# A four-block convolution network on one core: borders cleared alone, an up layer's weights prepared a stage earlier, x blocks loaded first, and loops written out

## The reference

```python
# L0: windowed attention, 8x8 windows, 8 heads, and an MLP with a hidden width of 768
h = layernorm(xw, ln1_g, ln1_b);  q, k, v = split(h @ qkv_w)
a = softmax(q k^T * scale) v @ proj_w + proj_b + xw
x = gelu(layernorm(a, ln2_g, ln2_b) @ fc1_w + fc1_b) @ fc2_w + fc2_b + a
# L1: Sobel edges in x and y, a 1x1 convolution of 384 to 192 channels, layernorm, gelu, residual
x = x + gelu(layernorm(conv1x1(edges(x))) * ln_w + ln_b)
# L2: 7x7 depthwise convolution, layernorm, up layer (w1) to 768, gelu, response norm, down layer (w2)
y = gelu(layernorm(depthwise7x7(x, dw_w) + dw_b) @ w1 + b1)
x = x + (grn_gamma * (y * nx) + grn_beta + y) @ w2 + b2     # nx from sums of y^2 over each image
# L3: 13x13 depthwise convolution and six dilated ones, each with a batch norm, summed
```

## Time and profile before

| | |
|---|---|
| median of 3 runs | 3580.73 us (3580.53 to 3581.01) |
| the profiled execution | 3581.64 us, of which the span from the first to the last instruction 3579.5 us |
| mean granted TensorE clock | 0.98 of full speed |
| TensorE busy | 3423.4 us (96%) |
| VectorE, ScalarE, GpSimd busy | 2389.3 (67%), 1790.2 (50%), 1080.1 us (30%) |
| transfers | 554.97 MB, 155 GB/s over the span |

### The profile page before, as it was taken

One profiled execution on the slowest core, in us unless ns is written; L12 is line 12 of the kernel. 1 busy time (PEld: TensorE's weight loads), 2 busy tenths in 40 slices (PEclk: granted clock), 3 DMA queues, 4 the chain that ended last, 5 costly groups with the idle time before them and its releaser, 6 DMA issues. The chain is left out here.

```text
span 3579.5 us, 95798 instructions
## 1 busy us (share of the span) xinstructions
PE 3423.4 (96%) x31958; PEld 3312.3 (93%) x31958; DVE 2389.3 (67%) x5936; ACT 1790.2 (50%) x5312; POOL 1080.1 (30%) x1951
## 2 busy tenths in 40 slices
PE   7999999999799999999969969989999899989999
PEld 6888888888699999999969969989999899989999
DVE  5777777777556666666659979979999311125554
ACT  4666666666444444444426657659999200002222
POOL 3233333333244444444425520014444223320000
PEclk9999999999899999999989989999999899999999
DMA  1455566610011111111158865537777788877775
GB/s 34 123 197 192 198 239 235 233 58 23 23 34 51 51 51 51 50 51 51 50 141 256 247 188 198 196 124 201 198 198 199 221 253 253 251 228 228 227 227 174
DMA packets 472671, 554.97 MB, mean 155 GB/s; under 512 B 78259, under 2 KB 331957, under 8 KB 472373
## 3 DMA queue, kind: packets, MB, share of 16 engines
q1 hardware_dynamic: 447028, 531.65, 49.3%
q10 hardware_dynamic: 25344, 19.27, 1.7%
HBM read 392.56 MB, written 271.52 MB: 186 GB/s over the span
## 5 line engine op out<-in xcount | busy, mean ns | idle before, releaser
L1325 PE MATMUL PS<-dw_grid,dw_mats 128*128 128x196 f32 (+1 forms) x3840 | 624.0, 326 | 37.0 <-DVE dw_mats L1266 37.0
L1325 PEld LDWEIGHTS PS<-dw_grid,dw_mats 128*128 128x128 f32 x3840 | 623.5, 191 | 37.5 <-DVE dw_grid L1262 37.5
L1297 ACT ACTIVATE dw_res<-PS,dw_brow 128x196 f32<-128x196 f32 x192 | 81.5, 424 | 699.3 <-PE PS L1325 699.3
L981 PE MATMUL PS<-mlp_w,mlp_hid 128*128 128x192 f32 x2352 | 414.0, 326 | 0.5 <-ACT mlp_hid L796 0.5
L1262 DVE COPY dw_grid<-X 32x392 f32 (+3 forms) x480 | 290.3, 605 | 171.8 <-PE PS L1325 148.7
L1560 PE MATMUL PS<-gain,down_hid 128*128 128x192 f32 x2352 | 385.4, 328 | 3.6 <-DMA down_hid<-scratch_hid 3.6
L1560 PEld LDWEIGHTS PS<-gain,down_hid 128*128 128x128 f32 x2352 | 385.1, 191 | 3.9 <-DMA down_hid<-scratch_hid 3.9
L981 PEld LDWEIGHTS PS<-mlp_w,mlp_hid 128*128 128x128 f32 x2352 | 378.3, 190 | 0.8 <-ACT mlp_hid L796 0.8
L796 ACT ACTIVATE mlp_hid<-PS,mlp_b 128x256 f32<-128x256 f32 x588 | 247.0, 471 | 110.8 <-PE PS L787 110.8
L1187 PE MATMUL PS<-sobel_wf,sobel_edge 96*128 96x192 f32 (+1 forms) x1568 | 261.0, 328 | 29.2 <-DVE sobel_edge L1122 28.9
L1187 PEld LDWEIGHTS PS<-sobel_wf,sobel_edge 96*128 96x128 f32 (+1 forms) x1568 | 257.3, 191 | 32.9 <-issue 32.8
(11 more groups left out here) (217 smaller groups left out, 9284.2 us busy)
## 6 DMA issues: line engine op xcount, KB each, us to landing
scratch_hid<-hid_hid SPq DMA_DIRECT2D x196, 384.0 KB, 3.7
down_hid<-scratch_hid SPq DMA_DIRECT2D x196, 384.0 KB, 4.0
scratch_wide<-scratch_taps SPq DMA_DIRECT2D x64, 960.0 KB, 5.3
dw_raw<-scratch_wide SPq DMA_DIRECT2D x96, 640.0 KB, 4.3
scratch_wide<-scratch_taps SPq DMA_DIRECT2D x64, 768.0 KB, 4.7
dw_raw<-scratch_wide SPq DMA_DIRECT2D x96, 512.0 KB, 3.3
sobel_xv<-scratch_v SPq DMA_DIRECT2D x56, 420.0 KB, 5.0
scratch_u<-mlp_u SPq DMA_DIRECT2D x56, 378.0 KB, 3.0
```

What stands on the lines that cost most here:

```text
L981: last = nc.tensor.matmul(psD[i], hid[:, p.buf(2), m, i * 128:(i + 1) * 128], w2[:, m, :], start=(m == 0), stop=(m == MC - 1))
L1325: last = nc.tensor.matmul(dst[:, :, ys, :], m, src, start=(i == 0), stop=(i == len(steps) - 1))
```

## The change

Four edits, and nothing else of the computation changes.

1. In `attention`, SyncE issues x blocks 0 to 3 before it waits for the memset and loads the weights; the taps follow the weights, then x from block 4 on.
2. In `depthwise`, GpSimd clears only columns 0 and 7 of `grid`, and then rows 0 and 14 of it (7x7 stage), or, for the 13x13 stage, the rows 0, 1, 22 and 23 of `mats`; `mats` of the 7x7 stage is no longer cleared. In the 7x7 stage the second memset waits for the first.
3. The up layer's weights (`UpWeights`, taken out of `NormUp`) are loaded and prepared in the 7x7 stage: SyncE loads at step 4, TensorE makes the bias products at step 16 after a wait for all results before, VectorE splits at step 16 and adds the bias at step 17. The bias products lie in the last bank, beside the results of the convolution. `hidden` then only waits for weights that are there. `mlp` does the same as before.
4. `run_steps` is gone; every use of it is `unrolled`. The `Fori` loops that SyncE has in `mlp` and `sobel` stay.

```diff
@@ attention, SyncE
+            for j in range(4):
+                body(Step(0, j, 2 * NB))
             w = a["L0_conv_qkv_w"]
             sp.wait_ge(q["cleared"], 1)
...
-            for j in range(NB):
+            taps.load(sp)
+            for j in range(4, NB):
                 body(Step(0, j, 2 * NB))
-                if j == 3:
-                    taps.load(sp)
@@ class UpWeights (load as it was in NormUp)
+    def shift_bias(self, pe, raw):
+        pe.wait_ge(self.q["loaded"], 16 * (1 + 3 * len(self.PACKED)))
+        for m in range(MC):
+            cols = slice(m * 128, (m + 1) * 128)
+            self.nc.tensor.matmul(self.psB[:, m:m + 1], raw[:, 0, cols], self.gb[:, 1, 0:1], start=True, stop=False)
+            last = self.nc.tensor.matmul(self.psB[:, m:m + 1], raw[0:64, 1, cols], self.gb[0:64, 1, 1:2], start=False, stop=True)
+        last.then_inc(self.q["shift"], 1)
+    def ready(self, eng):
+        eng.wait_ge(self.q["w1_ready"], 2)
+    def split(self, dve, raw):
+        dve.wait_ge(q["loaded"], 16 * (1 + 3 * len(self.PACKED)))
+        split_weights(nc, dve, q["high"], ...).then_inc(q["w1_ready"], 1)
+    def bias(self, dve):
+        dve.wait_ge(self.q["shift"], 1)
+        self.nc.vector.tensor_tensor(self.b1[:, :], self.b1[:, :], self.psB, ALU.add).then_inc(self.q["w1_ready"], 1)
@@ depthwise, SyncE, in body
+                if w1 and t.n == 4:
+                    w1.load(sp, w1raw, a["L2_conv_w1"], a["L2_conv_b1"], a["L2_conv_ln_w"], a["L2_conv_ln_b"])
@@ depthwise, GpSimd
-            nc.gpsimd.memset(grid[:, :, :, :, :, :], 0.0).then_inc(q["cleared"], 1)
-            nc.gpsimd.memset(mats[:, :, :, :, :, :], 0.0).then_inc(q["cleared"], 1)
+            lines = grid[:, :, :, :, :, :].rearrange("p r c i y x -> p (r c i y) x")
+            nc.gpsimd.memset(lines[:, :, 0:BX + 1:BX], 0.0).then_inc(q["cleared"], 1)
+            if tall:
+                kernels = mats[:, :, :, :, :, :].rearrange("p r c h y x -> p (r c h) (y x)")
+                edges = view(kernels[:, 0, 0:1], [[rows * 16, 4 * R], [22 * 16, 2], [1, 32]])
+            else:
+                edges = view(grid[:, 0, 0, 0, 0, 0:1], [[(BY + 1) * (BX + 1), 2 * IMG * R], [BY * (BX + 1), 2], [1, BX + 1]])
+                pool.wait_ge(q["cleared"], 1)
+            nc.gpsimd.memset(edges, 0.0).then_inc(q["cleared"], 1)
@@ depthwise, VectorE, end of body
+                if w1 and t.n == 16:
+                    w1.split(dve, w1raw)
+                if w1 and t.n == 17:
+                    w1.bias(dve)
@@ depthwise, TensorE, in body
                 pe.wait_ge(q["mats"], b.n + 1)
+                if w1 and t.n == 16:
+                    pe.wait_ge(q["result"], t.n * 2)
+                    w1.shift_bias(pe, w1raw)
+                if w1 and t.n == 19:
+                    w1.ready(pe)
@@ hidden
-            n.load(sp, w1raw, a["L2_conv_w1"], ...)
-            body(Step(0, 0, U))
-            body(Step(0, 1, U))
-            n.weights(dve, w1raw)
-            dve.wait_ge(n.q["w1_ready"], 2)
-            run_steps(dve, NP, U, HEAD, LAG, body, 2)
+            unrolled(NP, LAG, body)
...
-            n.transpose(pe, Step(0, 0, U), swapped=True)
-            n.shift_bias(pe, w1raw)
+            w1.ready(pe)
@@ every stage but attention, every engine
-            run_steps(pe, CP, U, HEAD, 0, body)
+            unrolled(CP, 0, body)
```

More of the change, by code:

```diff
@@ L91, in turn @@
         return self.g * (self.unroll // ring) + self.j // ring
-def run_steps(eng, count, unroll, head, lag, body, start=0):
-    assert (count - head) % unroll == 0
-    for j in range(start, head):
-        body(Step(0, j, unroll))
-    with eng.Fori(0, (count - head) // unroll) as g:
-        for j in range(unroll):
-            body(Step(g, head + j, unroll))
-    for j in range(count, count + lag):
-        body(Step(0, j, unroll))
 def unrolled(count, lag, body, start=0):
@@ L681, in __init__ @@
         self.psT = PS[:, 3, :]
-        self.psB = PS[:, 4, 0:MC]
-        self.q = {x: s.sem(x) for x in ("ready", "loaded", "w1_ready", "shift", "high", "stats", "aggr", "var_ok", "rstd",
-                                        "xn_ready", "xt", "h_high", "h_ready", "up", "gelu")}
-    def load(self, eng, raw, w, b, g, shift):
-        eng.dma_start(self.b1[:, :], b.rearrange("(m p) -> p m", m=MC)).then_inc(self.q["loaded"], 16)
-        for at_, rows, slot in self.PACKED:
-            eng.dma_start(raw[at_, slot, :], w[rows, :]).then_inc(self.q["loaded"], 16)
-            for i, vector in enumerate((g, shift)):
-                eng.dma_start(self.gb[at_, i, slot:slot + 1], vector[rows].rearrange("(p o) -> p o", o=1)).then_inc(self.q["loaded"], 16)
+        self.q = {x: s.sem(x) for x in ("ready", "stats", "aggr", "var_ok", "rstd", "xn_ready", "xt", "h_high", "h_ready", "up", "gelu")}
     def constants(self, pool):
@@ L700, in constants @@
         pool.wait_ge(self.q["ready"], 4)
-    def shift_bias(self, pe, raw):
-        pe.wait_ge(self.q["loaded"], 16 * (1 + 3 * len(self.PACKED)))
-        for m in range(MC):
-            cols = slice(m * 128, (m + 1) * 128)
-            self.nc.tensor.matmul(self.psB[:, m:m + 1], raw[:, 0, cols], self.gb[:, 1, 0:1], start=True, stop=False)
-            last = self.nc.tensor.matmul(self.psB[:, m:m + 1], raw[0:64, 1, cols], self.gb[0:64, 1, 1:2], start=False, stop=True)
-        last.then_inc(self.q["shift"], 1)
-        pe.wait_ge(self.q["w1_ready"], 2)
-    def weights(self, dve, raw):
-        nc, q = self.nc, self.q
-        dve.wait_ge(q["loaded"], 16 * (1 + 3 * len(self.PACKED)))
-        split_weights(nc, dve, q["high"], (raw[:, 0, :], raw[:, 1, :]), (self.gb[:, 0, 0:1], self.gb[:, 0, 1:2]),
-                      (self.wa[0][:, :], self.wb[0][:, :]), (self.wa[1][:, :], self.wb[1][:, :])).then_inc(q["w1_ready"], 1)
-        dve.wait_ge(q["shift"], 1)
-        nc.vector.tensor_tensor(self.b1[:, :], self.b1[:, :], self.psB, ALU.add).then_inc(q["w1_ready"], 1)
     def stats(self, dve, b):
@@ L1188, in body, with depthwise @@
                     last.then_inc(q["fused"], 1)
-            run_steps(pe, NS, U, HEAD, 0, body)
-def depthwise(nc, tag, turn, q, loaded, wide, bias, X, PS, out, expanded, stack):
+            unrolled(NS, 0, body)
+def depthwise(nc, tag, turn, q, loaded, wide, bias, X, PS, out, expanded, stack, a=None, w1=None):
     s = Scope(nc, tag, stack)
@@ L1210, in depthwise @@
     stored = s.sems("stored", 2) if out is not None else None
+    w1raw = s.sb("w1raw", [128, 2, HID]) if w1 else None
     def ps(b, c):
@@ L1267, in body @@
                 last.then_inc(q["mats"], 1)
-            run_steps(dve, CP, U, HEAD, 0, body)
+                if w1 and t.n == 16:
+                    w1.split(dve, w1raw)
+                if w1 and t.n == 17:
+                    w1.bias(dve)
+            unrolled(CP, 0, body)
         @block.scalar
@@ L1433, in _ @@
             pe.wait_ge(n.q["ready"], 4)
-            n.transpose(pe, Step(0, 0, U), swapped=True)
-            n.shift_bias(pe, w1raw)
+            w1.ready(pe)
             def body(t):
                 p = t.back(2)
-                if p.inside(NP) and not (p.fixed and p.n == 0):
+                if p.inside(NP):
                     n.transpose(pe, p, swapped=True)
```

102 lines of the change are left out of this document (58 added, 44 removed).

## The result

The changed kernel takes **3566.77 us** (median of 6 runs, 3565.47 to 3568.88), the kernel before on the same chip 3581.16 (6 runs, 3580.53 to 3586.21). The ratio is 0.9958, with a 95% interval of 0.9945 to 0.9971: 15 us faster (14.4 by the medians), where the sum said 21.1. The time is 7 us above the forecast of 3560 and inside its range. The profiled execution took 3567.07 us, 1.8 around its span; against that of before it is 14.6 us shorter.

A forecast was written before the change was run, and what follows sets the result against it. The prediction took TensorE, busy for 3423.4 of 3579.5 us, to bound the kernel. Its terms summed to -21.1, taking 3581.64 to 3560.5, by the median 3559.6, rounded to 3560 us; the range was 3552 to 3569.

The forecast's parts named there:

- 1. x first: Attention's start: with x blocks issued ahead of the weights, bias matmuls start at 13.2 to 13.4 instead of 20.34, -7.0 us.
- 2. loops: MLP, Sobel: Writing loops out removes the MLP's five issue stops, -7.6 us, and some weight-load idling in the Sobel stage, -1.5.
- 2. streaming, and the other loops: From Sobel on, 75 newly fetched instruction blocks cost +1 us (0 to +5); the other stages' loops give 0.
- term 5: 7x7 stage: preparing the up layer's weights there costs +4.1 us, a stop and 24 one-column matmuls at step 16.
- term 6: Up layer's start: with weights already prepared, normalization waits only for transposes and rstd values, -8.2 us.
- 7. clock at the stages' starts: 7x7 and 13x13 starts: TensorE's half-clock stretches after long stops change in length, +1 us (-3 to +3).
- 5.7 us after the raw issue: 7x7 stage's start: a sign that the first matmul comes 5.7 us after the stage's raw issue, grid copies long over.
- A: From Sobel on, fetching the new blocks eats the gain, slower than before; 12 stops give 3590 us; chance 0.05.
- B: 7x7 stage: the preparation costs VectorE's lead, which does not come back, 5 us more, 3565; chance 0.10.
- C: Attention's start: the x blocks delay the weights, giving 3 us instead of 7, 3564; chance 0.08.
- D: Convolution starts: the memsets were all of it, raw transfers land sooner, 6.9 us more gained, 3553; chance 0.05.
- E: MLP: written-out loops do nothing, another wait stands where the branch stood, 3567 us; chance 0.03.

The follow-up runs named there:

- experiment 8: The kernel before with only the first four x blocks issued ahead of attention's weights; 3572.52 us, ratio 0.9980.
- experiment 6: The kernel before with all its loops written out and nothing else changed; 3567.84 us, ratio 0.9971.
- experiment 7: The kernel before with only the narrow border clears of the two convolutions; 3575.06 us, ratio 0.9993.
- experiment 3: The changed kernel with the early preparation undone, the up layer's memory laid out as in the kernel before; 3560.04 us, ratio 0.9944.
- experiment 9: The changed kernel with weights prepared in the up layer's stage, their tiles left at the changed kernel's address; 3566.77 us, ratio 0.9965.
- experiment 10: The changed kernel with bias products spread over two steps and the sums' tile allocated ahead of the weights; 3554.13 us, ratio 0.9931.
- experiment 12: The changed kernel with one edit, the sums of squares' tile allocated ahead of the up layer's weights; 3560.52 us, ratio 0.9949.
- late: Same run as experiment 3: the changed kernel with the early preparation undone; 3560.04 us, ratio 0.9944.
- Spread: Same run as experiment 10: bias products over two steps, sums' tile ahead of the weights, against the changed kernel; 3554.13 us, ratio 0.9931.
- x first: Same run as experiment 8: the kernel before with only the first four x blocks ahead of attention's weights; 3572.52 us, ratio 0.9980.
- late, same place: Same run as experiment 9: the changed kernel with weights prepared late, tiles at the changed kernel's address; 3566.77 us, ratio 0.9965.
- Experiment 5: The changed kernel run again on another chip, nothing edited; 3565.76 us, ratio 0.9959.
- experiment 2: The changed kernel with two unused tiles, 48 bytes a partition before the up layer's weights and 16 behind; 3567.60 us (one run).

## Why the prediction was right, and where it was not

By its own terms, with what each measured in the place it named:

| term | forecast | measured | from |
|---|---|---|---|
| 1. x first | -7.0 | -6.8 | experiment 8, first dense matmul |
| 2. loops: MLP, Sobel | -7.6, -1.5 | -8.1, -1.0 | experiment 6 |
| 2. streaming, and the other loops | +1 | -3.0 (-1.3) | experiment 6, the rest of its table (of its ratio) |
| 3. borders, 7x7 | -1.2 | -1.6 | experiment 7, idle time 27.16 to 25.52 |
| 4. borders, 13x13 | -1.7 | -2.0 | experiment 7, idle time 9.85 to 7.87 |
| 5. preparation, its price | +4.1 | +6.5 | step 16 of the changed kernel |
| 6. preparation, its gain | -8.2 | -8.2 | first two columns |
| 7. clock at the stages' starts | +1 | +0.7 | first 32 matmuls: 7x7 8.4 to 8.2, 13x13 6.8 to 7.6 |
| not in the sum | | +8.6 | experiments 3, 9, 10, 12 |

The measured column adds up to -14.9, against -14.4 by the medians. That the time stayed in the range was in part luck: 8.6 that the sum did not have and 2.4 too little in term 5 are 11 us, and 2 to 4 of them were taken back by the other loops, which had been put at nothing.

**The direction and most terms stood.** The bias matmuls began at 13.52 where 13.3 was forecast, after the last weight and no longer after x; all five MLP stops went; both convolutions wait for their raw transfer and no longer for a memset. (The sign "5.7 us after the raw issue" did not fit the forecast's own sum, in which it is 7.53 - 1.2 = 6.3; measured were 6.03.) A strided memset costs 0.94 us for 480 elements, 2.3 times the full one's 0.86 ns each, inside the bound, and the copies had the room.

**The step that failed is the one left out**: term 6 moved the preparation and took its matmuls, waits and transfers into account, but not that the weights' tiles change their place. To be alive during the 7x7 kernel they are allocated ahead of it, so the gains (9,216 bytes), the constants (768) and the sums (2,368 with rounding) no longer lie under them and they stand 12,352 bytes lower. With the tiles so each of 2940 up matmuls takes 2.9 ns more: (406.1 - 397.6) / 2940. Against before it shows as 6.9, since the stage was 1.4 shorter with the loops written out (experiment 6). The Trainium skill, page "SBUF — State Buffer", section "Who interferes with whom", says that TensorE and ScalarE never wait on anyone. The trace agrees in so far as no wait appears in it; but the same matmuls ran at two paces by the tiles' addresses alone, so no wait did not mean no loss here. Whether other engines' accesses are behind the slower pace is not shown.

**Term 5 was mis-sized**, by two pieces. The 24 one-column matmuls take 3.71 / 24 = 0.155 us each, and not half of what they took at half clock (3.1 / 24 = 0.129 by the forecast): 0.6 more. And the clock fell to 0.50 behind them for 3.4 us, 1.8 us of time; before it fell TensorE had stopped for 0.88 us and then run only one-column matmuls. In all 0.9 + 3.7 + 1.8, and 0.15 for the modelled end of the matmul before. In two portions of 12, without the stop, it did not fall, and the price was 3.7. The stop itself was 0.9 (forecast 1.0). The term on the clock had looked only at the stages' starts. Another 1.2 us of the 7x7 stage's 7.7 over "late" lie in its first 32 matmuls, 8.2 us for 7.0, where the clock is low after the start. These are not shown to be a price of the preparation: the six kernels without it in that stage took 6.8 to 8.4 us for them.

**So what is the early preparation worth?** In one piece, -8.7 + 7.7 = -1.0 by the table against "late" with good addresses in both: 0.9949 against 0.9944 measured, nothing. Spread, -8.7 + 4.3 = -4.4: 0.9931, an interval that still overlaps that of "late". Without the first 32 matmuls of the 7x7 stage it is -2.2 and -5.0. As it was made, at the worse address, the stage table adds 8.6: "late" is 7.8 us ahead of the changed kernel by the profiled executions and 0.14% by the ratios, which their intervals alone would not settle.

**The rivals.** A (fetching eats the gain): none of the 90 blocks from Sobel on made TensorE wait; VectorE has more "issue" time than before (70 us for 24, in the MLP), and it is hidden. (A block lasts 1769 / 91 = 19.4 us there and 956 / 120 = 8.0 in attention, 2.4 times as long and not three.) The Trainium skill, page "Runtime: NRT & Kernel Launch", section "Instruction fetch mechanics", has blocks streamed ahead with the crossing mostly hidden; with those 90 blocks the trace agrees. B (VectorE's lead): no wait of TensorE for matrices after step 16; "DVE dw_mats" ended one wait in that stage, the start's. C: the last weight was issued 0.8 us later, not 4. D: the transfer landed 5.1 us after its issue, 5.3 before; nothing more was to be had. E: the MLP gave its 7.6. The times that E and B forecast, 3567 and 3565, were nearer to the measured one than the forecast itself, and neither for its reason.

## What to carry to other kernels

When a tile is made to live longer or earlier, its address is part of the change: compare the pace of a stage's matmuls, start to start, before and after, also where no stop is seen, and try another allocation order before giving a result to the schedule. Short matmuls put into a full stream cost their own time and, here, in one piece behind a stop, the clock after them; split them into portions between the long ones, where no result has to be waited for. A gain at one stage's start is worth what is left after the price in the stage that now does the work, so measure the part undone, not only done.

## What the runs showed of the hardware

**One stop in attention, and the clock, make most of its differences.** Fourteen profiled executions, of kernels with the same attention matmuls, took 936.3 to 946.3 us for the stage. In each TensorE has one long stop for "issue" ahead of the same group of matmuls, near 120 to 130 us, for 0.8 to 3.9 us. "x first" has 0.8 and 936.3; "late, same place" 3.9 and 946.3, for the clock then stood at 0.50 for 10 us. In ten of the fourteen it stood there for 3.4 to 10.2 us behind the stop, and in three, the kernel before among them, for 3.4 us more near the stage's end, from 947 to 954 on (the last line). With the stop and half of these stretches taken off, 935 to 938 us are left. The waits of these two, the window behind the second's stop, and the window near the end of attention in the kernel before:

```profile
PE PS L588 <- issue: 0.8, 1, 0.8
```

```profile
PE PS L576 <- issue: 3.9, 1, 3.9
```

```profile
122.00:132.00 10.00, 9.51 (x91) 8.70 (x91) 4.07 (x11) 3.35 (x10) 1.56 (x3) 0.50 0.05 11
```

```profile
949.90:953.30 3.40, 3.33 (x25) 2.71 (x25) 0.92 (x3) 0.43 (x2) 0.00 (x0) 0.50 0.00 0
```

The changed kernel's -3.0 in attention is this and not the change: 1.1 of the stop (1.4, before's 2.5) and 1.7, half of those 3.4 us at the end, which it did not have. Experiment 5, the same kernel, had them, a stop of 3.1, and 944.2 for the stage. No branch stands there, and the profile names no releaser; that a block of instructions came late is likely and not shown.

**The same program has two paces in the MLP**, 0.1173 and 0.1194 us from matmul to matmul, for a whole stage or part of it (5.9 us between the extremes); the up layer's pace was the same, to 0.0003 us, in every execution at one address. Equal attention differed by up to 9.2 us among the ten executions of kernels with x first and written-out loops (937.1 to 946.3), so by an estimate from these two figures 15 us can lie between equal programs' profiled executions, as much as this change is worth: why single profiles had to be read stage by stage here and not by their totals.

**Left open**: what in the addresses decides the pace. 0.1199 was seen with the weights at the changed kernel's address, 0.1168 at 12,352 and at 2,368 bytes above it, 0.1185 with the two pads of experiment 2; no rule was tried on these four points. Gains and sums moved along with the weights in all of them.
